# Self-attention in a fused three-block kernel: where the value and key projections stand among the transposes

## What is computed

```python
def cross_attention(x, ctx, wq, wk, wv, wo, bo):      # 20 heads of 64
    q = jnp.einsum('bne,ef->bnf', x, wq).reshape(B, N, HEADS, DHEAD).transpose(0, 2, 1, 3)
    k = jnp.einsum('bme,ef->bmf', ctx, wk).reshape(B, M, HEADS, DHEAD).transpose(0, 2, 1, 3)
    v = jnp.einsum('bme,ef->bmf', ctx, wv).reshape(B, M, HEADS, DHEAD).transpose(0, 2, 1, 3)
    scores = jnp.einsum('bhnd,bhmd->bhnm', q, k) * SCALE
    attn = jax.nn.softmax(scores, axis=-1)
    out = jnp.einsum('bhnm,bhmd->bhnd', attn, v)
    out = out.transpose(0, 2, 1, 3).reshape(B, N, HEADS * DHEAD)
    return jnp.einsum('bnf,fe->bne', out, wo) + bo

x = cross_attention(layer_norm(x, g1, be1), layer_norm(x, g1, be1), wq1, wk1, wv1, wo1, bo1) + x
```

## Time and profile before

| what | value |
|---|---|
| median of 3 runs | 1027.56 us (1027.3 to 1028.69) |
| the profiled execution | 1029.73 us, span of its instructions 1027.9 us |
| busy: PE, DVE, ACT, POOL | 95%, 67%, 57%, 37% of the span |
| steady loop of self-attention | from 175.6 to 767.4 us of the span |
| granted TensorE clock, mean | 0.995 |

### The profile page before, as it was taken

The page is one execution under the profiler, slowest core; times in us unless marked ns, Lnnn a source line. Parts: engine busy times, 40 slices in busy tenths (PEclk is TensorE's granted clock), DMA queues, the critical chain, the costliest instruction groups (busy, mean ns, idle before and its releaser), DMA issues.

```text
span 1027.9 us, 17534 instructions
## 1 busy us (share of the span) xinstructions
PE 978.5 (95%) x6376; PEld 706.1 (69%) x6376; DVE 690.7 (67%) x1171; ACT 591.1 (57%) x1332; POOL 378.9 (37%) x493
## 2 busy tenths in 40 slices
PE   7999978999999999999999999999999989999998
PEld 4566666656667666667666668666556689998887
DVE  2767646776774676774777674776645789999463
ACT  2666635667763766764666764666644455455442
POOL 2676623344342434332444332343321034444120
PEclk9999989999999999999999999999999999999999
DMA  6400050000000000000000000000000330000000
GB/s 135 94 1 1 1 148 1 1 1 2 1 1 2 1 1 2 1 1 1 1 1 2 1 1 2 1 1 2 1 1 25 100 95 1 1 1 1 1 26 26
DMA packets 25371, 17.64 MB, mean 17 GB/s; under 512 B 8566, under 2 KB 24102, under 8 KB 25286
## 3 DMA queue, kind: packets, MB, share of 16 engines
q1 hardware_dynamic: 25285, 16.52, 6.4%
HBM read 11.26 MB, written 1.31 MB: 12 GB/s over the span
## 4 chain that ended last, share of the span: by engine, by line
PE 64%; DVE 10%; ACT 5%; issue 4%; POOL 1%; DMA 1%; SPq 0%; DVEq 0%; ACTq 0%; POOLq 0%
PE banks L409 13%; PE banks L396 12%; PE banks L382 11%; PE banks L416 4%; PE banks L224 3%; ACT sa_probs L499 3%; PE banks L1645 2%; PE banks L227 2%; PE banks L226 2%; PE banks L225 2%; PE banks L1937 2%; DVE ca_top L1780 2%; PE banks L232 2%; DVE ca_probs L1785 1%; DVE sa_negmax L571 1%
## 5 line engine op out<-in xcount | busy, mean ns | idle before, releaser
L643 POOL TENSOR_SCALAR sa_probs<-sa_probs,sa_inverse 128x512 f32<-128x512 f32 x320 | 216.8, 692 | 361.7 <-DVE sa_inverse L575 361.7
L499 ACT ACTIVATE sa_probs<-banks,sa_negmax 128x512 f32<-128x512 f32 x320 | 215.6, 685 | 125.7 <-DVE sa_negmax L571 125.6
L571 DVE TENSOR_REDUCE sa_negmax<-banks 128x2 f32<-128x1024 f32 x160 | 188.7, 1218 | 10.4 <-PE banks L382 7.4
L396 PEld LDWEIGHTS banks<-ident,sa_probs 128*128 128x128 f32 x1280 | 144.5, 141 | 55.6 <-issue 27.6
L396 PE MATMUL banks<-ident,sa_probs 128*128 128x128 f32 x1280 | 172.6, 275 | 9.9 <-ACT sa_turned L510 5.8
L580 DVE COPY sa_turned<-banks 128x512 f32<-128x512 f32 x160 | 110.1, 688 | 75.6 <-PE banks L396 75.6
L409 PE MATMUL banks<-sa_turned,sa_v 128*64 128x512 f32 x640 | 155.0, 605 | 0.0
L382 PE MATMUL banks<-sa_k_parts,sa_q_parts 64*128 64x512 f32 x960 | 133.2, 408 | 1.9 <-ACT sa_probs L499 1.9
L510 ACT COPY sa_turned<-banks 128x512 f32<-128x512 f32 x160 | 94.2, 589 | 58.2 <-PE banks L396 56.3
L382 PEld LDWEIGHTS banks<-sa_k_parts,sa_q_parts 64*128 64x128 f32 x960 | 83.9, 184 | 30.4 <-issue 14.1
L409 PEld LDWEIGHTS banks<-sa_turned,sa_v 128*64 128x64 f32 x640 | 38.7, 136 | 74.3 <-issue 73.1
(11 more groups left out here) (218 smaller groups left out, 1727.2 us busy)
## 6 DMA issues: line engine op xcount, KB each, us to landing
w_o<-in_L_xattn_wo SPq DMA_DIRECT2D x2, 800.0 KB, 9.1
out<-x SPq DMA_DIRECT2D x4, 320.0 KB, 2.4
w_q_t<-in_L_xattn_wq_t SPq DMA_DIRECT2D x1, 1120.0 KB, 10.4
fold_values<-ca_turned SPq DMA_DIRECT2D x5, 192.5 KB
x<-in_x SPq DMA_DIRECT2D x1, 960.0 KB, 5.8
fold_values<-ca_probs SPq DMA_DIRECT2D x4, 192.5 KB
w_q_t<-in_L_xattn_wq SPq DMA_DIRECT2D x1, 640.0 KB, 6.2
w_o<-in_L_xattn_wk SPq DMA_DIRECT2D x1, 640.0 KB, 9.2
```

The costliest lines, as they stand in the source:

```text
L396: last = pe.transpose(b_turn[e][:, q * P:(q + 1) * P], probs[:, j % 2, e, q, k * P:(k + 1) * P], ident[:])
L499: act.activation(probs[:, j % 2, e, q, :], b_scores[u % 2][:, e, :], ACT.Exp, bias=negmax[:, u % RING, e:e + 1], accum_out=total[:, u % RI ...
L571: dve.tensor_reduce(negmax[:, u % RING, :], b_scores[u % 2], AX_X, ALU.max, negate=True).then_inc(s_max.sem, 1)
L643: pool.tensor_scalar(probs[:, j % 2, e, q, :], probs[:, j % 2, e, q, :], inverse[:, u % RING, e:e + 1], 1.0, ALU.mult, ALU.mult).then_inc( ...
```

## The change

In even double units TensorE now runs the first turn right behind `pv`, the value projection between the two turns, and the key projection behind the second turn. VectorE's `copy_v` moves behind the copy of the first turn, and ScalarE's `round_k` behind its copy of the second turn. Odd double units keep their order; no instruction is added or taken away.

```diff
@@ TensorE, batch @@
                     if d >= 1:
                         pv(b, 2 * d - 2)
                         pv(b, 2 * d - 1)
-                    if d % 2 == 0:
-                        over(next_v, b, d // 2 + 2, NPAIR, more)
...
                     if d % 2 == 0:
-                        over(next_k, b, d // 2 + 2, NPAIR, more)
+                        over(next_v, b, d // 2 + 2, NPAIR, more)
                     else:
                         over(next_q, b, d // 2 + 3, NPAIR, more)
                     turns(b, 2 * d + 1)
+                    if d % 2 == 0:
+                        over(next_k, b, d // 2 + 2, NPAIR, more)
                     for i in range(2):
                         over(scores, b, 2 * (d + LEAD + 1) + i, NU, more)
@@ ScalarE, batch @@
                     copy_turned(b, 2 * d)
+                    if d % 2 == 1:
+                        over(round_q, b, d // 2 + 3, NPAIR, more)
+                    copy_turned(b, 2 * d + 1)
                     if d % 2 == 0:
                         over(round_k, b, d // 2 + 2, NPAIR, more)
-                    else:
-                        over(round_q, b, d // 2 + 3, NPAIR, more)
-                    copy_turned(b, 2 * d + 1)
@@ VectorE, batch @@
+                    copy_turned(b, 2 * d)
                     if d % 2 == 0:
                         over(copy_v, b, d // 2 + 2, NPAIR, more)
-                    copy_turned(b, 2 * d)
                     if d > 0 or b == 0:
                         over(inverses, b, m + 1, NU, more)
```

## The result

| | before | after |
|---|---|---|
| median | 1027.72 us (4 runs, 1027.3 to 1028.69) | 1045.52 us (4 runs, 1045.07 to 1046.43) |
| profiled execution | 1029.73 us | 1045.07 us |
| span, granted clock | 1027.9 us, 0.995 | 1043.3 us, 0.995 |

The ratio is 1.0173 (95% interval 1.0155 to 1.0191): the new order makes the kernel 1.7% slower. The two profiled executions differ by 15.3 us.

The account below looks back on a forecast made before the run. TensorE was taken to set the pace. Ordinary pairs (4.8 us) and the other pairs together add 15.4 us to the profiled 1029.73, giving 1045.1; less 2.2 for the median, 1043.0 us, range 1034 to 1050.

Parts of the forecast that it names:

- both waits: Even unit: second half of the second turn waits 0.28 us for ScalarE's copy; odd unit: later maxima cost 0.30 us.
- The old wait: Even unit before the change: the key projection waits for VectorE's value copy by at least 0.10 us.
- Part 2: Even unit: ScalarE's copy of the first turn is late; second turn's second half at 4.48, not 4.20, 0.28 us wait.
- Part 3: Even unit, key projection last: starts at 4.90, takes 1.04, scores at 5.93; unit 0.03 to 0.05 us longer.
- Part 4: Odd unit: rest of the key delays maxima to about 7.35, some 0.44 us late; unit grows by 0.30 us.
- No growth from pair to pair: Next even unit: maxima start in their old place, so each pair costs the same.
- Special pairs: Totals: d = 6 and 7 2.4 us, 8 and 9 3.7, 11 and 13 0.2, 15 1.9, 0 and 1 2.4.
- The sum: Whole loop: ordinary and other pairs together cost 15.4 us; 1045.1 for the profiled execution, median 1043.0 after taking off 2.2.
- Part 1: Even unit, first turn at 1.87: GpSimd's last product ends over a microsecond before the unit begins, so no wait.
- Only the first new wait counts: Rival: the odd unit takes the later maxima without loss; 5 us slower, 1032.6; chance 0.08.
- the delay does not end with the pair: Rival: late exponentials make the next even unit's copy late by another 0.3 us; 25 us, 1052; chance 0.07.
- The wait is removed and nothing replaces it (faster): Rival: even unit's scores come 0.13 us earlier, 38 times is 5 us: 1022.6; chance 0.04.

Follow-up runs that it names:

- the first experiment: Changed kernel with ScalarE's copy_att moved behind its copy of the first turn in even units; 1037.78 us, ratio 1.0106.
- the first three experiments: Changed kernel with copy_att behind ScalarE's copy (1037.78 us), with the rest of the key behind the maxima (1035.62 us), and with both edits (1029.05 us).
- second experiment: Changed kernel with VectorE's rest of the key moved behind both maxima of the next unit (d = 0, 2, 4, 6, 8, 16, 18); 1035.62 us, ratio 1.0079.
- e7: Kernel before with the layer norm's statistics (d = 6) and scaling step (d = 7) moved ahead of VectorE's copy of the second turn; 1025.37 us, ratio 0.9976.

## Why the prediction was right

The forecast was 1043.0 us in a range of 1034 to 1050; measured were 1045.5. The mechanism and both waits are shown by experiment: each edit takes away its own growth of the even or of the odd unit, and both together bring an ordinary pair to 13.71 us against 13.76 before the change. The whole loop is back at 584.8 against 585.1, but that owes 2.4 us to d = 6 to 8.

- **The old wait** of the key projection for the value copy is gone in the changed kernel: the copy ends at 311.82, 0.24 ahead of the projection. It comes back as soon as ScalarE's copy is out of the way. In the first experiment the value copy ends at 309.78, the key projection starts at 309.84, and the turn in front of it takes 0.95 us to there, as before the change. So no run shows a pair with neither wait.
- **Part 2** was exact: second half of the second turn at 4.48 in ordinary units, and 5.06 in d = 8 (5.07 foretold).
- **Part 3** was too low. The key projection starts at 4.89 (4.90 foretold), but the scores start 1.11 us behind it and not 1.04, and the unit ends 0.02 later still. I took the 1.04 from the key projection going over into transposes. Its last matmul starts at 312.84 and the scores 0.33 later, where two of its own are 0.24 apart. The even unit costs 0.14 and not 0.04.
- **Part 4** was too high by about as much. The maxima start at 7.33 (7.35 foretold), but the odd unit they belong to begins at 7.60, so they are 0.31 late and not 0.44, and the unit grows by 0.19 and not 0.30. The pair: 0.32 us against 0.34. That the two errors cancel in the pair is no second piece of luck: how long the pair takes goes by when the maxima start, which was foretold within 0.02 us, and what the even unit takes longer the same maxima are less late. The late maxima in the old order bear out the slack: 0.47 us of lateness cost 0.34, and 0.47 - 0.17 + 0.04 is 0.34.
- **No growth from pair to pair:** the maxima of every ordinary even unit start 0.58 ahead of it, as before.
- **Special pairs,** measured (foretold): d = 6 and 7 0.59 (0.59), d = 8 and 9 0.89 (0.93), d = 11 and 13 0.12 to 0.14 (0.03, the even unit's share once more), d = 15 0.44 (0.47), d = 0 and 1 0.56 (0.60). The sum counts four pairs of d = 0 and 1. Batch 0 has no update of `x` to wait for, and its d = 0 stands ahead of the loop; three pairs show the 0.56.
- **The sum** was 15.4 us; the loop grew by 15.0 and the profiled executions differ by 15.3. The medians differ by 17.8. What was off by 2.5 us is the last step, the 2.2 us that I took off because the profiled execution of before stood that much above its median. It did so at a mean granted clock of 0.995, with the stretch of 0.50 at 950.2 us. Of the 55 executions of the kernel before that ran beside the experiments, 51 have 0.997 on average. Of the changed kernel's four, three have 0.995 and one 0.993, and its profiled one stands 0.45 below its own median. The stretch was the exception before and is the rule after, so it should not have been taken off.
- **Part 1** held in the loop, not in d = 0 of batch 0, where the first turn now stands idle for 1.45 us (176.07 above) and the clock falls directly behind. The other kernels with the new order there, the first three experiments, show the same idle time, 1.44 us. Two of them have the same stretch behind it, and their loops start at 182.7 and 182.8 us. The second experiment has its stretch at 956.3 instead and starts at 180.8. None of the 22 executions of these four kernels has a mean clock of 0.997. That speaks for the new order as what brings the stretch, but it isn't shown: in the kernel before with the rest of the key of d = 6 late, seven of eleven executions have 0.995 too.
- **The rivals.** "Only the first new wait counts" fell with the second experiment, "the delay does not end with the pair" with the maxima's place in even units. "The wait is removed and nothing replaces it (faster)": with `copy_att` out of the way and the maxima in their place, pairs are 0.05 shorter, not 0.13. The key projection starts at 4.70 (4.71 foretold), but the scores 1.14 us behind it and not 1.04 (309.84 to 310.98 in the first experiment).
- The rule that the queues of ScalarE, VectorE and GpSimd are in order ("PSUM — Partial Sum Buffer", "Engine vs sequencer instructions", the Trainium skill) is borne out by the second experiment: only a new program order let the maxima pass the rest of the key.

What stays open: why a seam between the key projection and the scores costs 0.09 us. The two differ in tiling (128 rows against 64 in the rows), and turn to scores shows a step of 0.20 against 0.11 as well, but no run separated this. The traces of the eleven kernels also start this loop between 180.2 and 183.2 us. Five have a single stretch of 0.50 ahead of it, 6.8 us long at 147 to 149 us, and start at 180.2 to 181.3. The three with a second one at 176 us start at 182.7 to 183.2, and the three with two of 3.4 us at 150 and 160 us at 181.6 to 181.7. What brings these stretches and the remaining scatter was not tested.

## What to carry to other kernels

When a step is moved behind another on the busiest engine, follow its results through the queues of the engines that read them: here moving the key by one turn cost TensorE itself about 0.1 us, at the seam to the scores, but on VectorE it stood in front of work that was ready and on the loop's longest chain. Give each wait its slack in us before the move (0.17 us decided this case), and look for the instruction that stands directly ahead of the chain's: on VectorE the layer norm's statistics were nearly free one copy earlier. A gap on the busiest engine is worth only what the next release behind it leaves. And when two medians are compared by way of a profiled execution, look at the granted clock of all their executions first.

## What the runs showed of the hardware

Two kinds of VectorE instructions that only touch SBUF ran slower beside GpSimd, down to half speed: the scaling step 2.02 us for four where GpSimd multiplied probabilities, 1.18 where it hardly did, 0.63 for two where it was idle; the spare addition 1.38 instead of 0.68 beside GpSimd's bias addition. A third kind did not: the layer norm's statistics, with one input, took 0.98 us for four with GpSimd at work beside three of them (e7, batch 1), and 0.99 with GpSimd idle before the change:

```profile
372.17 0.98 DVE L135 BATCH_NORM_STATS2 ln_stats<-x 128x6 f32<-128x160 f32 x4
372.45 0.69 POOL L643 TENSOR_SCALAR sa_probs<-sa_probs,sa_inverse 128x512 f32<-128x512 f32 x1 [0.81 <-DVE sa_inverse L575]
```

Copies out of PSUM did not slow down either. From the timeline of the changed kernel, with GpSimd at work for the whole of the copy:

```profile
309.69 1.37 POOL L643 TENSOR_SCALAR sa_probs<-sa_probs,sa_inverse 128x512 f32<-128x512 f32 x2 [3.46 <-DVE sa_inverse L575]
309.76 0.69 DVE L580 COPY sa_turned<-banks 128x512 f32<-128x512 f32 x1 [0.26 <-PE banks L396]
```

The value copy at 311.13, which GpSimd's work does not touch, took 0.69 as well. The Trainium skill ("SBUF — State Buffer", section "Who interferes with whom") says that the two engines share a pair of SBUF ports, that a VectorE instruction with two SBUF inputs contends with a GpSimd instruction that reads SBUF, that one in a two-port mode contends too, and that one with at most one SBUF input outside these modes does not. In the case of the two-port mode, it says, the engine that comes second is blocked. The addition (two inputs), the statistics (one) and the copies (none in SBUF) agree with this. Whether the scaling step ran in a two-port mode no row shows, and no run here separated the port from other causes.

The start of VectorE's next instruction lies 0.60 to 0.61 us behind a 0.68 to 0.69 us one, so rows overlap by 0.08 us; sums over full durations would have been 0.08 too long at each step.
